# A two-layer attention kernel on one core: transposes three steps behind the scores, and the tables that follow it

## Chip, core and metric

The kernel runs on one core of one Trainium2 chip. The time is that of the device in microseconds (us) for one execution, from the first to the last thing that the core does. A core has five engines with a queue of instructions each: TensorE (PE in the rows; its loads of weights stand apart as PEld), VectorE (DVE), ScalarE (ACT), GpSimd (POOL) and SyncE (SP), which here issues nearly all DMAs. Every engine works through its own queue in order, and an instruction may wait for semaphores that other engines raise. The granted clock of TensorE was 0.993 of full speed over the profiled execution.

## What is computed

The input x is (4, 16, 16, 256) in fp32. Two attention layers are added to it, each on a group-normalised input:

```
x = x + L0(gn(x))     # 8 heads over the 16 rows, 256 tokens, relative bias, softmax over 256
x = x + L1(gn(x))     # 16 heads, 4 chunks of 64 tokens, keys of the chunk and the one before it

L0: xi = w_in . x;  q, k = w_qk . xi;  sim = (q k + bias[buckets]) / 4;  out = w_out . (softmax(sim) v), v = xi
L1: q, k, v = w_qkv . x;  attn = softmax over the chunk's 128 keys of q k / 4;  out = w_out . (attn v)
gn: mean and variance over 16 x 16 positions and 8 neighbouring channels, 32 groups
```

## The kernel before

**Units, blocks and steps.** The work is cut into 8 units: units 0 to 3 are the first layer (A) for batches 0 to 3, units 4 to 7 the second layer (B) for the same batches. A unit has 8 blocks of scores of 128 x 512. All engines run the same loop `for t in range(STEPS)`, STEPS = 8 x 8 + 12, and each puts into its own queue what the tables give to step t. Nothing but these tables sets the order in which an engine meets its instructions; semaphores set when it may go on.

**A block through the engines.** In step t TensorE makes the scores of block t (`scores`, L572 in A, L584 in B; one of two banks). VectorE adds the bias and takes the maximum (A, L952), or takes the maximum and subtracts it (B, L956 and L963). In A the maximum is subtracted on GpSimd (L362, in step t - LAG + 2). TensorE transposes a block at step t + LAG (`shifted`, L594 and L603), and ScalarE takes its exponential in the same step (L1191, PT). Two steps ahead of each block ScalarE prepares the queries: QM for every block in A (L1171), QP for every second block in B (L1182).

**A unit's end.** Its numbers in FINISH are steps counted from the unit's first block: values (L663, L673; TensorE, by halves of a unit), first transposes of the unnormalised output (L689, L693), second transposes of the normalised one (L700), output product (L706, L710). Between them ScalarE copies values out (OS, L1198, in the step of the values), VectorE divides (RC and ON, L972 to L980, in the step of the first transposes), ScalarE copies the second transposes (OT, L1206, in their step), and VectorE adds the residual one step after the output product (L989, L995). A unit of A has its ends once, a unit of B twice, for two halves. The bracketed pairs in the tables are these two halves; where a unit of A does it once, the second number counts.

**A unit's beginning.** The steps in TIMES_A, counted from the unit's first block and so negative, are those of the projection to heads XR, of Q, of K and of V (which in A is a transposition of XF). VectorE scales XR (XF, L855) in XR's step, ScalarE rounds it (XRh, L1108) in the same step, VectorE makes its low part (XRl, L866) one step later. The low parts of queries and keys (Qst and KL, L875 and L879) come one step after Q and K, the copy of V (VA, L906) one step after V. For layer B the six numbers are the transposes of X (XT), the two matmuls over groups for mean and variance (GM, GV), and Q, K, V. ScalarE writes the normalised input as a rounded XTh and a full XT (rows show XT as Sq) at GV + 1, GpSimd its low part XTl at GV + 2 (L370). ScalarE and VectorE split Q and K into high and low parts (L1134, L1139, L885); SP writes Q's and K's parts to memory and loads them back in another layout (L290, L295, L296), Q before K: store Q, store K, load Q, load K. ScalarE copies V (VB, L1150) one step after V.

**Buffers.** The score banks and the banks of the transposes are two each and alternate. F and G are one bank each: XR, K and XT use F; Q, V, GM and GV use G, in A as in B. The banks O, one for each half, hold values, both transposes and output product in turn. The subtracted blocks (SB) lie in a ring of six, the queries QM in one of four, PT holds the eight blocks of a unit.

**On ScalarE the order inside a step is:** squares and weights (first ten steps only), exponential, QM or QP, XRh, XTh and XT, high parts, VB, then OT, then OS. The two loops that give it, exponential and queries left out:

```
for step, when in enumerate((GV_B + 1, Q_B, K_B)):
    for i in due(t, when, IN_B):
        projected(i, step)
...
for i in due(t, t2[1], units_a(units)):
    normalised(i, 0)
```

## Time and profile before

| | |
|---|---|
| median of 3 runs | 175.76 us (175.17 to 175.86) |
| profiled execution | 175.02 us, span 173.1 us |
| busy | PE 150.5 (87%), DVE 110.8 (64%), ACT 108.4 (63%), POOL 53.0 (31%) |
| PE busy from 60 to 157 us | 88.7 of 97.0 us |
| PE busy from 157 us on | 10.9 of 16.1 us |
| chain that ended last | PE 59%, DVE 15%, ACT 11%, issue 7%, POOL 3%, DMA 3% |

A busy share tells how full an engine is, not whether it is waited for. For that the timeline has, ahead of an instruction, the time that its engine sat idle and who released it. The 16 us at the end are the drain: no scores are left to make, and the last unit goes through its ends one after the other. The first 60 us hold the start, in which statistics, weights and the first units share the engines.

### The profile page before, as it was taken

The numbers are of one execution on the slowest core, as the hardware profiler recorded it, in microseconds if no ns is written. First come the engines' busy times: TensorE is split into PE (matmuls) and PEld (weight loads), VectorE is DVE, ScalarE is ACT, GpSimd is POOL, SyncE is SP. The second block draws the span as 40 slices with busy tenths as digits, with TensorE's granted clock in tenths as the row PEclk, the third lists the DMA queues.
The fourth block names the chain that finished last, engine by engine and source line by source line (L and its number), as shares of the span: only waits on it lengthen the run. The fifth ranks groups of instructions, "written<-read, shape, count | busy, mean of one in ns | idle before, by whom it ended". The sixth has DMA issues, their size and how long they took to land.

```text
span 173.1 us, 4283 instructions
## 1 busy us (share of the span) xinstructions
PE 150.5 (87%) x1582; PEld 129.6 (75%) x1582; DVE 110.8 (64%) x326; ACT 108.4 (63%) x218; POOL 53.0 (31%) x106
## 2 busy tenths in 40 slices
PE   7989889769979799899989798998999898979872
PEld 7568769648868579887888677987899787868651
DVE  1645477955483776348646886799667779678220
ACT  1428417955856378737893769766976968775520
POOL 0302532959953245924590122003200200000000
PEclk9999999999999999999999999999999999999997
DMA  5409900000000000079505890369307980010101
GB/s 176 146 6 296 304 4 6 0 0 4 2 2 0 0 4 2 13 174 239 184 4 130 220 256 4 83 167 242 125 0 189 239 239 29 8 34 0 64 26 40
DMA packets 8564, 15.84 MB, mean 92 GB/s; under 512 B 1208, under 2 KB 5688, under 8 KB 7776
## 3 DMA queue, kind: packets, MB, share of 16 engines
q1 hardware_dynamic: 7984, 15.22, 32.1%
q10 hardware_dynamic: 560, 0.35, 0.7%
q8 instruction: 13, 0.21, 0.5%
q14 instruction: 7, 0.06, 0.1%
HBM read 10.31 MB, written 5.26 MB: 90 GB/s over the span
## 4 chain that ended last, share of the span: by engine, by line
PE 59%; DVE 15%; ACT 11%; issue 7%; POOL 3%; DMA 3%; ACTq 1%; DVEq 0%
PE bank L572 6%; PE bank L584 6%; PE bank L603 5%; PE bank L552 5%; PE bank L663 5%; PE bank L673 4%; PE bank L710 4%; PE bank L594 4%; PE bank L561 3%; PE bank L479 3%; DVE NM L956 3%; POOL XTl L370 3%; DMA PT<-buckets 3%; ACT Sq L1127 2%; DVE SB L963 2%
## 5 line engine op out<-in xcount | busy, mean ns | idle before, releaser
L1191 ACT ACTIVATE PT<-bank 128x512 f32<-128x512 f32 x64 | 38.2, 598 | 23.7 <-PE bank L603 11.9
L952 DVE CUSTOM_DVE_ANT_0 SB<-bank,Tk 128x256 f32<-128x256 f32 x64 | 24.5, 420 | 20.3 <-PE bank L572 20.2
L362 POOL TENSOR_SCALAR SB<-SB,NM 128x256 f32<-128x256 f32 x64 | 29.9, 481 | 13.9 <-DVE NM L952 13.5
L956 DVE TENSOR_REDUCE NM<-bank 128x4 f32<-128x512 f32 x32 | 21.9, 685 | 13.2 <-PE bank L584 13.1
L963 DVE TENSOR_TENSOR SB<-bank,NM 128x512 f32<-128x512 f32 x32 | 22.1, 692 | 1.1
L572 PE MATMUL bank<-KH,QM 128*128 128x256 f32 x64 | 21.2, 351 | 0.7 <-ACT QM L1171 0.7
L584 PE MATMUL bank<-K,QP 96*128 96x128 f32 x128 | 20.7, 284 | 0.7 <-ACT QP L1182 0.7
L1182 ACT ACTIVATE QP<-Q,con 96x512 fp32r<-96x512 f32 x32 | 21.2, 713 | 0.0
L603 PE MATMUL bank<-con,SB 128*128 128x128 f32 x128 | 19.8, 278 | 0.0
L594 PE MATMUL bank<-con,SB 128*128 128x128 f32 x128 | 19.3, 273 | 0.0
L584 PEld LDWEIGHTS bank<-K,QP 96*128 96x128 f32 x128 | 17.0, 191 | 2.4 <-ACT QP L1182 0.9
L572 PE MATMUL bank<-KL,QM 128*128 128x256 f32 x64 | 17.8, 297 | 0.0
L1171 ACT ACTIVATE QM<-Qst,con 128x256 fp32r<-128x256 f32 x32 | 16.0, 506 | 0.5 <-DVE Qst L875 0.5
L572 PEld LDWEIGHTS bank<-KH,QM 128*128 128x128 f32 x64 | 13.2, 206 | 3.7 <-issue 3.4
L594 PEld LDWEIGHTS bank<-con,SB 128*128 128x128 f32 x128 | 14.6, 140 | 0.0
L603 PEld LDWEIGHTS bank<-con,SB 128*128 128x128 f32 x128 | 13.6, 141 | 0.1
L1198 ACT ACTIVATE OS<-bank 128x256 f32<-128x256 f32 (+1 forms) x16 | 7.8, 490 | 9.1 <-PE bank L663 5.7
L572 PEld LDWEIGHTS bank<-KL,QM 128*128 128x128 f32 x64 | 13.3, 208 | 0.2
L385 POOL COPY VB<-VB 64x256 f32<-64x256 f32 x4 | 1.6, 390 | 31.5 <-ACT VB L1150 31.5
L700 PE MATMUL bank<-con,ON 128*128 128x128 f32 x24 | 5.1, 296 | 5.1 <-DVE ON L980 4.6
L663 PE MATMUL bank<-PT,VA 128*32 128x256 f32 x128 | 8.6, 385 | 0.9 <-ACT WoT L1097 0.9
L673 PEld LDWEIGHTS bank<-PT,VB 128*32 128x32 f32 x512 | 7.5, 110 | 1.8 <-ACT PT L1191 1.2
(142 smaller groups left out, 274.3 us busy)
## 6 DMA issues: line engine op xcount, KB each, us to landing
q_terms<-WQK SPq DMA_DIRECT2D x16, 128.0 KB, 2.2
k_terms<-KHL SPq DMA_DIRECT2D x16, 128.0 KB
Q<-q_terms SPq DMA_DIRECT2D x4, 512.0 KB, 5.4
K<-k_terms SPq DMA_DIRECT2D x4, 512.0 KB, 5.6
Tk<-bias_rows SPq DMA_DIRECT2D x4, 384.0 KB, 4.7
X<-x SPq DMA_DIRECT2D x4, 256.0 KB, 4.5
Q<-q_terms SPq DMA_DIRECT2D x4, 256.0 KB, 5.9
K<-k_terms SPq DMA_DIRECT2D x4, 256.0 KB, 6.1
```

Of the source, the lines that this page charges most:

```text
L362: last = nc.gpsimd.tensor_scalar(rows_of, rows_of, -1.0, NM[:, i % 2, 2 * u + nt:2 * u + nt + 1], ALU.mult, ALU.add)
L572: last = nc.tensor.matmul(s[:, nt * CH:(nt + 1) * CH], queries[:, nt * P:(nt + 1) * P], keys[:, i % 2, u // 4, :], start=(nt == 0 and keys ...
L584: last = nc.tensor.matmul(bank[S_BANK + u % 2][:, a * P:(a + 1) * P], QP[0:ROWS, c % QRING, a, g].rearrange("p v n -> p (v n)"), window, s ...
L594: last = nc.tensor.transpose(z[:, s * CH + nt * P:s * CH + (nt + 1) * P], below[:, nt * CH + s * P:nt * CH + (s + 1) * P], ident)
L603: last = nc.tensor.transpose(z[:, a * P:(a + 1) * P], below[:, a * P:(a + 1) * P], ident)
L663: last = nc.tensor.matmul(o[32 * hh:32 * hh + 32, 0:CH], VA[:, i % 3, mt, 4 * half + hh, :], PT[:, 4 * half + hh, mt * CH:(mt + 1) * CH], ...
L952: last = V.tensor_tensor_reduce(SB[:, idx % SRING, nt * CH:(nt + 1) * CH], half, Tk[:, u, nt * P:nt * P + CH], 1.0, LOWEST, ALU.add, ALU.m ...
L956: V.tensor_reduce(NM[:, i % 2, 4 * u:4 * u + 4], s[:].rearrange("p (h m) -> p h m", h=4), AX.X, ALU.max).then_inc(max_ready, 1)
L963: V.tensor_tensor(SB[:, idx % SRING, :].rearrange("p (h m) -> p h m", h=4), bank[S_BANK + u % 2][:].rearrange("p (h m) -> p h m", h=4), NM ...
L1171: A.activation(QM[:, idx % MRING, :], Qst[:, i % 2, u // 4, :].bitcast(F32), ACT.Copy, scale=con[:, C_PAIR + u % 4:C_PAIR + u % 4 + 1]).th ...
L1182: last = A.activation(QP[0:ROWS, c % QRING, :, :, v, :].rearrange("p a g n -> p (a g) n"), Q3[0:ROWS, b % 2, :, :, c * CHUNK:(c + 1) * CHU ...
L1191: A.activation(PT[:, u, :], bank[Z_BANK + u % 2][:], ACT.Exp, scale=-SCALE if is_a(i) else SCALE).then_inc(p_ready, 1)
```

## The change

LAG goes from 4 to 3: the transposes and the exponential of a block come three steps after its scores. STEPS stays. The steps of the units' beginnings and ends change with it. For unit 0 its first and second transposes and output product stand at 13, 15, 16; for units 1 to 3 values and first transposes come one step sooner, the second transposes keep their step 14, and the output product comes one step sooner, at 15. For layer B values, first transposes and output products come one step sooner, the second transposes keep their steps (the last unit's second half comes one sooner). For unit 1, K and V come ahead of Q in the queue, in units 2 and 3 too. In layer B the group matmuls, Q and V come one step later, K stays, so that Q and K share a step. The waits follow the new order in the banks: Q waits for the copy of V, V for XF and the former unit's queries, XRh and XRl for the former unit's Q in place of its K.

```diff
@@ -239,16 +239,17 @@
 
 
 
-        LAG = 4
+        LAG = 3
         STEPS = UNITS * BLK + 12
         IN_A, IN_B = range(BATCH), range(BATCH, UNITS)
-        TIMES_A = [(range(1, 2), (-6, -4, -3, -2)), (range(2, 3), (-5, -3, -3, -2)), (range(3, BATCH), (-9, -8, -8, -7))]
-        XT_B, GM_B, GV_B, Q_B, K_B, V_B = -14, -13, -12, -9, -8, -7
-
-
-        FINISH = [(IN_A, (9, 12), (13, 13), (14, 14), (16, 16)),
-                  (range(BATCH, UNITS - 1), (10, 13), (12, 15), (13, 16), (15, 18)),
-                  (range(UNITS - 1, UNITS), (10, 13), (12, 15), (13, 16), (14, 17))]
+        TIMES_A = [(range(1, 2), (-6, -4, -5, -5)), (range(2, 3), (-5, -3, -4, -4)), (range(3, BATCH), (-9, -7, -8, -8))]
+        XT_B, GM_B, GV_B, Q_B, K_B, V_B = -14, -12, -11, -8, -8, -6
+
+
+        FINISH = [(range(1), (9, 12), (13, 13), (15, 15), (16, 16)),
+                  (range(1, BATCH), (8, 11), (12, 12), (14, 14), (15, 15)),
+                  (range(BATCH, UNITS - 1), (9, 12), (11, 14), (13, 16), (14, 17)),
+                  (range(UNITS - 1, UNITS), (9, 12), (11, 14), (13, 15), (14, 16))]
 
         def units_a(units):
             return [i for i in units if i in IN_A]
@@ -479,23 +480,24 @@
                         last = nc.tensor.matmul(f[:, 0:CH], WinK[:, t, :], Xc[:, i, t, :], start=(t == 0), stop=(t == TT - 1))
                     last.then_inc(xr_done, 1)
                 if step == 1:
-                    pe.wait_ge(v_ready, v_total(i - 1))
-                    pe.wait_ge(xr_ready, i + 1)
+                    pe.wait_ge(v_ready, v_total(i))
                     for n, (w, v) in enumerate(((WQh, XRh), (WQl, XRh), (WQh, XRl))):
-                        if v is XRl:
-                            pe.wait_ge(xrl_ready, i + 1)
                         for t in range(2):
                             last = nc.tensor.matmul(f[:, t * CH:(t + 1) * CH], w[:, t, :], v[:, ::-1],
                                                     start=(n + t == 0), stop=(n == 2), skip_group_check=True)
                     last.then_inc(q_done, 1)
                 if step == 2:
+                    pe.wait_ge(xr_ready, i + 1)
                     for n, (w, v) in enumerate(((WKh, XRh), (WKl, XRh), (WKh, XRl))):
+                        if v is XRl:
+                            pe.wait_ge(xrl_ready, i + 1)
                         for t in range(2):
                             last = nc.tensor.matmul(f[:, t * CH:(t + 1) * CH], w[:, t, :], v[:],
                                                     start=(n + t == 0), stop=(n == 2), skip_group_check=True)
                     last.then_inc(k_done, 1)
                 if step == 3:
-                    pe.wait_ge(q_ready, i + 1)
+                    pe.wait_ge(q_ready, max(i, 1))
+                    pe.wait_ge(xs_ready, i + 1)
                     for m in range(2):
                         last = nc.tensor.transpose(f[:, m * P:(m + 1) * P], XF[:, m * P:(m + 1) * P], ident)
                     last.then_inc(v_done, 1)
@@ -530,7 +532,10 @@
                     last.then_inc(xt_done, 1)
                 if step == 1:
                     pe.wait_ge(agg_ready, b + 1)
-                    pe.wait_ge(v_ready, v_total(i - 1))
+                    if b == 0:
+                        pe.wait_ge(q_ready, i)
+                    else:
+                        pe.wait_ge(v_ready, v_total(i - 1))
                     nc.tensor.matmul(m[:, 0:CT], con[:, C_GRP:C_GRP + P], agg[:, :, 0], start=True, stop=True).then_inc(gm_done, 1)
                 if step == 2:
                     pe.wait_ge(mom_ready, b + 1)
@@ -862,7 +867,7 @@
                 if i == 1:
                     dve.wait_ge(part_k, 2)
                 if i >= 2:
-                    dve.wait_ge(k_done, i - 1)
+                    dve.wait_ge(q_done, i - 1)
                 V.tensor_tensor(XRl[:], XF[:], XRh[:].bitcast(F32), op=ALU.subtract).then_inc(xrl_ready, 1)
 
             def queries_keys(i, which):
@@ -1104,7 +1109,7 @@
                         if i == 1:
                             act.wait_ge(part_k, 2)
                         if i >= 2:
-                            act.wait_ge(k_done, i - 1)
+                            act.wait_ge(q_done, i - 1)
                         A.activation(XRh[:], XF[:], ACT.Copy).then_inc(xr_ready, 1)
                     if which == 1:
                         act.wait_ge(q_done, i)
```

**ScalarE, steps 29 to 31 (before).** PT is the exponential, QM and QP are queries, XTh and Sq the normalised input of unit 5, OT the copy of unit 2's second transposes.

```order
L1191 ACTIVATE PT<-bank 128x512
L1171 ACTIVATE QM<-Qst,con 128x256
L1127 ACTIVATE XTh<-bank,gnb,grs 128x256 x2
L1127 ACTIVATE Sq<-bank,gnb,grs 128x256 x2
L1191 ACTIVATE PT<-bank 128x512
L1182 ACTIVATE QP<-Q,con 96x8x64 x2
L1206 ACTIVATE OT<-bank 128x256
L1191 ACTIVATE PT<-bank 128x512
L1134 ACTIVATE WQK<-bank 128x512
```

**The same place after the change:**

```order
L1176 ACTIVATE QM<-Qst,con 128x256
L1196 ACTIVATE PT<-bank 128x512
L1187 ACTIVATE QP<-Q,con 96x8x64 x2
L1132 ACTIVATE XTh<-bank,gnb,grs 128x256 x2
L1132 ACTIVATE Sq<-bank,gnb,grs 128x256 x2
L1211 ACTIVATE OT<-bank 128x256
L1196 ACTIVATE PT<-bank 128x512 x2
L1187 ACTIVATE QP<-Q,con 96x8x64 x2
L1139 ACTIVATE WQK<-bank 128x512
```

OT of unit 2 stood a step after XTh and XT (Sq); now it stands right behind them, with the step's queries QP in front of them.

**TensorE, steps 38 to 40 (before).** K,QP are scores, con,SB a block's transposes, con,ON the second transposes of unit 3, OT,WoutK its output product, XTh and WTh the Q and then the K of unit 6.

```order
L584 MATMUL bank<-K,QP 128x128 x4
L603 MATMUL bank<-con,SB 128x128 x4
L700 MATMUL bank<-con,ON 128x128 x2
L584 MATMUL bank<-K,QP 128x128 x4
L603 MATMUL bank<-con,SB 128x128 x4
L552 MATMUL bank<-XTh,WTh 128x256 x4
L552 MATMUL bank<-XTh,WTl 128x256 x4
L552 MATMUL bank<-XTl,WTh 128x256 x4
L584 MATMUL bank<-K,QP 128x128 x4
L603 MATMUL bank<-con,SB 128x128 x4
L552 MATMUL bank<-XTh,WTh 128x256 x4
L552 MATMUL bank<-XTh,WTl 128x256 x4
```

**After, steps 37 to 39 and the start of 40:**

```order
L589 MATMUL bank<-K,QP 128x128 x4
L608 MATMUL bank<-con,SB 128x128 x4
L542 MATMUL bank<-mom,con 128x2
L589 MATMUL bank<-K,QP 128x128 x4
L608 MATMUL bank<-con,SB 128x128 x4
L705 MATMUL bank<-con,ON 128x128 x2
L589 MATMUL bank<-K,QP 128x128 x4
L608 MATMUL bank<-con,SB 128x128 x4
L711 MATMUL bank<-OT,WoutK 128x256 x2
L589 MATMUL bank<-K,QP 128x128 x4
L608 MATMUL bank<-con,SB 128x128 x4
L557 MATMUL bank<-XTh,WTh 128x256 x4
```

The output product stood behind both Q and K, two steps after the second transposes; now it stands one step after them, and Q and K follow it together.

**TensorE, steps 3 to 5 at the start (before).** KH,QM and KL,QM are scores, con,VB a transposition of layer B's weights, Part,avg means for the group norm of units 2 and 3, XRh and XRl with WQK the projections of unit 1.

```order
L572 MATMUL bank<-KH,QM 128x256
L572 MATMUL bank<-KL,QM 128x256
L572 MATMUL bank<-KH,QM 128x256
L572 MATMUL bank<-KL,QM 128x256
L594 MATMUL bank<-con,SB 128x128 x4
L450 MATMUL bank<-Part,avg 128x64
L727 MATMUL bank<-con,VB 128x128 x4
L488 MATMUL bank<-XRh,WQK 128x256 x4
L488 MATMUL bank<-XRl,WQK 128x256 x2
L572 MATMUL bank<-KH,QM 128x256
L572 MATMUL bank<-KL,QM 128x256
L572 MATMUL bank<-KH,QM 128x256
```

**After, from step 3's transposes on:**

```order
L599 MATMUL bank<-con,SB 128x128 x4
L495 MATMUL bank<-XRh,WQK 128x256 x4
L495 MATMUL bank<-XRl,WQK 128x256 x2
L502 MATMUL bank<-con,XF 128x128 x2
L577 MATMUL bank<-KH,QM 128x256
L577 MATMUL bank<-KL,QM 128x256
L577 MATMUL bank<-KH,QM 128x256
L577 MATMUL bank<-KL,QM 128x256
L599 MATMUL bank<-con,SB 128x128 x4
L451 MATMUL bank<-Part,avg 128x64
L732 MATMUL bank<-con,VB 128x128 x4
L486 MATMUL bank<-XRh,WQK 128x256 x4
```

K and V (con,XF) of unit 1 and one more block's transposes now stand ahead of the means and of the weights' transposition.

## Rows read from the trace of the kernel before

**Rows 1.** TensorE's timeline, first score matmuls: start us, us, engine, line, operation, tiles

```profile
59.12 0.39 PE L572 MATMUL bank<-KH,QM 128*128 128x256 f32 x1
...
73.51 0.47 PE L572 MATMUL bank<-KH,QM 128*128 128x256 f32 x1
...
91.43 0.75 PE L584 MATMUL bank<-K,QP 96*128 96x128 f32 x4
...
110.51 0.75 PE L584 MATMUL bank<-K,QP 96*128 96x128 f32 x4
...
129.23 0.64 PE L584 MATMUL bank<-K,QP 96*128 96x128 f32 x4
...
156.06 0.64 PE L584 MATMUL bank<-K,QP 96*128 96x128 f32 x4
```

**Rows 2.** timeline of VectorE at the end

```profile
170.55 0.43 DVE L995 TENSOR_TENSOR Y<-bank,X 128x256 f32<-128x256 f32 x1 [2.14 <-PE bank L710]
```

**Rows 3.** chain that ended last: start us, us, engine and line

```profile
20.56 1.15 PE bank L572 x4
...
71.56 1.44 PE bank L552 x12
72.99 0.87 PE bank L706 x4
73.86 0.48 PE bank L572 x4
...
76.21 1.00 PE bank L663 x16
...
129.48 0.40 PE bank L584 x4
129.88 0.46 PE bank L603 x4
```

**Rows 4.** timeline, steps 3 to 9; in brackets idle before and its releaser

```profile
26.19 0.41 DVE L866 TENSOR_TENSOR XRl<-XF,XRh 128x256 fp32r<-128x256 f32 x1
...
26.33 0.43 PE L450 MATMUL bank<-Part,avg 128*128 128x64 f32 x2 [1.15 <-DVE Part L791]
...
38.11 1.07 PE L663 MATMUL bank<-PT,VA 128*32 128x256 f32 x16 [0.88 <-ACT WoT L1097]
```

**Rows 5.** timeline of TensorE and ScalarE, steps 29 and 30

```profile
82.45 0.39 PE L572 MATMUL bank<-KH,QM 128*128 128x256 f32 x1
...
83.66 0.60 ACT L1191 ACTIVATE PT<-bank 128x512 f32<-128x512 f32 x1 [0.69 <-PE bank L594]
...
84.55 1.02 ACT L1127 ACTIVATE XTh<-bank,gnb,grs 128x256 fp32r<-128x256 f32 x2
...
86.35 0.62 ACT L1191 ACTIVATE PT<-bank 128x512 f32<-128x512 f32 x1
...
86.83 1.34 ACT L1182 ACTIVATE QP<-Q,con 96x512 fp32r<-96x512 f32 x2
...
88.05 0.38 ACT L1206 ACTIVATE OT<-bank 128x256 f32<-128x256 f32 x1
```

**Rows 6.** timeline of GpSimd at step 30

```profile
86.56 1.27 POOL L370 TENSOR_TENSOR XTl<-Sq,XTh 128x512 fp32r<-128x512 f32 x1 [1.77 <-ACT Sq L1127]
```

**Rows 7.** timeline of SP's queue for unit 4

```profile
75.78 1.74 SPq L290 DMA_DIRECT2D k_terms<-KHL  x4
...
78.14 0.58 SPq L296 DMA_DIRECT2D Q<-q_terms  x1
79.70 0.53 SPq L295 DMA_DIRECT2D K<-k_terms  x1
```

**Rows 8.** DMA issues: KB each, median us from issue to landing

```profile
Q<-q_terms SPq DMA_DIRECT2D x4, 512.0 KB, 5.4
K<-k_terms SPq DMA_DIRECT2D x4, 512.0 KB, 5.6
```

**Rows 9.** TensorE at a second transposes of unit 6

```profile
153.78 0.44 PE L700 MATMUL bank<-con,ON 128*128 128x128 f32 x2 [1.15 <-DVE ON L980]
```

## The prediction

> **What bounds the kernel now.** I read the stretches by engine first, then the gaps on TensorE with what ended them, then the chain of waits, and ScalarE's and SP's own rows where a gap ended on them. TensorE (PE) works through nearly the whole span, so an instruction that moves counts only where PE waits for it, or where a wait goes. I measure in stretches of PE's rows, S(t) being the first score matmul of step t. S(18), S(25), S(33), S(41), S(49) and S(63) start at 59.12, 73.51, 91.43, 110.51, 129.23 and 156.06 [rows 1], and the last residual add ends at 170.98 [rows 2]. Between them PE does pieces of known length: scores 0.48 in layer A and 0.40 in B, a block's transposes 0.46, each of Q, K and V of layer B 1.44, a value product 1.00, an output product 0.87 [rows 3]. For the four transposes of X or of the unnormalised output I take 0.4, for the two of the normalised one 0.2, both by rule of three from the 0.46. PE's waits are what is left in a stretch, 1 to 3 us of each.
>
> **What costs nothing by itself.** No instruction is added or taken away. PE's work is constant, and the sum is one of waits. The transposes of a block now stand two whole steps behind its scores, at least 1.7 us by rows 3, and VectorE and GpSimd need less than that; I take 0, with +1 as the other bound.
>
> **The first ten steps.** K and V of unit 1 now stand at step 3, ahead of S(4), and K's last third needs XRl. On VectorE XRl stands behind the reductions of units 2 and 3 and ends at 26.60. Before, PE waited for the same reductions, but with only their means left to do: it goes on at 26.33 [rows 4]. Now K's rest (0.3), V (0.4), S(4) (0.5) and a block's transposes (0.45) stand after XRl and before these means and the weight transposes that ScalarE waits for: they come 1.95 us later. ScalarE then works without a gap up to step 9. It has K's copy and one exponential (0.5 each) behind it already, but meets the centring on GpSimd, which now stands behind a later block. Followed to step 9, the value product that starts at 38.11 [rows 4] comes 2.9 later. Bounds: 0 (the two early pieces pay for all) and +3.5; I take +2.9. From S(10) to S(18) I take 0: V no longer waits for Qst (about 1.2, twice), but Q waits for V's copy, which VectorE makes only after that step's maxima (0.9, twice), and K for XRl (0.3, twice).
>
> **The output product behind ScalarE's normalisation: the main term.** For units 1 to 3 the output product stands one step behind the second transposes in place of two, and it needs OT. ScalarE issues in that step the exponential, QM or QP, XTh and XT, and only then OT; before, XTh and XT stood one step earlier. The exponential starts 1.2 after its step's scores (82.45 to 83.66), it and QM hold 0.9, XTh with XT 1.8 (84.55 to 86.35), the exponential alone 0.5, QP 1.22 (86.83 to 88.05), OT 0.38 [rows 5]. So OT is there 1.2 + 0.9 + 1.8 + 0.4 = 4.3 after S(22), and with QP in place of QM 5.1 after S(30) and S(38). PE wants it after one step, the two small transposes and another step: 2.15 (1.97 in layer B). The waits are 2.2, 2.95 and 3.1. What goes in return is Q's wait for XTl, which ends at 87.83 [rows 6] and kept PE 0.7 to 1.1 each time; the output product now covers it.
>
> **Q and K by way of memory.** Q and K of layer B now stand in one step, so VectorE makes both low halves in the next one, Q's first. SP stores Q, then K, then loads Q. K's stores begin at 75.78, 2.27 after S(25), and take 1.74; Q's second load is issued at 78.14, K's first at 79.70, and such loads land 5.4 and 5.6 after issue [rows 7, 8]. Q's low half now ends where K's did (2.2), its stores take 1.75, and so K's begin at 3.95 and Q has landed at 11.65. ScalarE wants it at S(30) + 1.7 = 11.0: 0.65 late. Counted from S(33) it is 12.05 against 11.1: 0.95 late. Both stand in front of OT, whose waits become 3.65 and 4.1. K lands 14.3 after S(41) and S(49), where S(48) and S(56) want it at 12.7 and 12.55. XT at steps 26, 34 and 42 needs K's low half, at 2.8, 3.15 and 3.0 of its stretch, and is due at 2.0, 1.9 and 2.85: +0.8, +1.25, +0.15.
>
> **What goes.** The layer's group means now stand where ScalarE has no QP ahead of V's copy, and a piece of PE work covers their statistics: PE's waits of 0.5 to 1.4 there, 3 us in all, go. The second transposes of layer B stand two steps behind the first, so the wait for ON, 1.15 at 153.78 [rows 9] and the same one unit earlier, goes. After S(63) there is one step less to drain: walked with rows 3 and 5 the end comes 12.3 after S(63) starts, in place of 14.9.
>
> **Sum, now minus before.** To S(10) +2.9. S(18) to S(25), 14.4 before: work 13.1 (one value product more), wait 2.2, joints 0.8, 16.1: +1.7. S(25) to S(33), 17.9: S(30) at 9.3, output product 15.1 to 16.0, a step with Q, K and a value product 4.8, 20.8: +2.9. S(33) to S(41), 19.1: S(38) at 9.45, output product 15.5 to 16.4, a step with Q and K 3.8, 20.2 (one value product less): +1.1. S(41) to S(49), 18.7: S(48) at 14.3, XTl at 16.3, the rest of Q, K and two transposes 2.15, 18.4: -0.3. S(49) to S(63), 26.8: S(56) at 14.3 and seven steps of 12.2, 26.5: -0.3. Drain -2.6. Together +5.4. The profiled execution took 175.02 us, 1.9 more than its span, so 180.4; the three runs shown have their median 0.74 above it, which gives 181.2. I say 181.0.
>
> **A rule on the loads.** The 512 KB loads took 5.4 us to land [rows 8]. The Trainium skill (DMA: Bandwidth & Descriptors, Anatomy of one DMA) puts a transfer at about 2.0 us plus its bytes at 436 GB/s; for both loads of a pair, 768 KB, that estimate is 3.8 us, and by it Q and K would be in time everywhere and the sum some 3.6 smaller. The row decides for me.
>
> **Rivals.**
> *The loads are in time.* The 0.65 and 0.95 in front of OT go, and so do the 1.6 and 1.75 before S(48) and S(56), of which XTl takes 1.3 back: -3.6, 177.4. For it: the 5.4 was seen with other traffic around. Against it: the stores move by more than the margin that the loads had. Chance 0.17, with the cases in which only the start loses less.
> *The other side: OT is not waited for.* If PE comes to the output products of steps 23, 31 and 39 no earlier than ScalarE has OT, 9.95 us go and +5.4 becomes -4.5: 170.5, and 171.2 against the median. It turns faster by over 0.5% once these three waits total under 3.6 us. For it: the gains at the second transposes and in the drain are sure. Against it: ScalarE keeps its order, and XTl, which ends later still, would take 4.4 back, which ends at 175.7, no change. Chance 0.12 for faster, 0.08 for no change.
> *PE's clock falls.* The four scores of a step took 1.15 at 20.56 and take 0.48 at 73.86 [rows 3]: at the start, between gaps, PE runs at the lower of its levels (1.2 GHz), after steady work at the higher (2.4), while the granted clock reads full in both. Waits of 3.65 and 4.1 don't occur in the loop before. If they drop it, the 3.8 us of scores, Q and K behind each take up to twice as long: up to +7.6, and 184.8 at half of that. The Trainium skill (TensorE: Matmul & The Clock Gate, Part 1: The HAM clock gate) says that an idle array goes back to half its clock. Chance 0.13.
>
> **Numbers.** Forecast 0.50, with its own range 178.6 to 183.0; the rivals as above. 176.5 to 184.5 leaves out the other side and the worst of the clock. About 0.5% (0.9 us) is what a measurement tells from no change: faster 0.12, same 0.08, slower 0.80.
>
> **What would show it.** In the profile after: three output products of layer A (bank from OT and WoutK) with PE idle 2 to 4 us before them, released by OT, and XTh and XT right in front of OT on ScalarE; S(48) or S(56) released by K's load; no wait over 0.3 at the second transposes of the last two units; the last residual add ending 12 to 12.6 after S(63) starts; the first value product starting near 41. The forecast is wrong if the waits at the three output products total under 6 us, if the first value product starts before 39.5, or if K's load never releases the scores.

## The result, and the profile after

The changed kernel takes 196.32 us (median of 4 runs, 194.83 to 197.06) against 175.46 us before (4 runs, 175.13 to 175.86): a ratio of 1.118, 95% interval 1.110 to 1.125. Slower was right; 181.0 was 15 us too low, and 196.32 lies far outside the range. The profiled execution took 195.98 us, 20.96 more than that of before, with a span of 194.0.

The page after, engines' busy time and, in 40 slices of the span, the granted clock of TensorE in tenths:

```profile
PE 159.4 (82%) x1582; PEld 137.3 (71%) x1582; DVE 111.4 (57%) x326; ACT 109.4 (56%) x218; POOL 53.3 (27%) x106
...
PEclk9958699999999978999799996999859997599999
```

The clock row of the kernel before:

```profile
PEclk9999999999999999999999999999999999999997
```

PE makes the same 1582 instructions as before and is busy 159.4 us instead of 150.5. So about 8.9 us of the 20.9 in the span are not waits at all: the same matmuls took longer. The other 12.0 are idle time of PE. The clock row shows where the matmuls were slow: behind the start it dips five times. The low digits of the start itself are no loss against the kernel before, whose pieces there are as slow under a row that reads full (last section).

Stretches of the kernel after, from S(10) to S(18), S(25), S(33), S(41), S(49), S(56) and S(63); columns are length, busy PE, PEld, DVE, ACT and POOL with counts, granted clock, DMA share, GB/s:

```profile
39.82:59.96 20.14, 18.47 (x148) 14.94 (x145) 11.33 (x46) 11.78 (x25) 12.36 (x25) 1.00 0.01 2
59.96:77.81 17.85, 15.85 (x133) 13.77 (x131) 9.10 (x43) 11.20 (x23) 8.50 (x16) 0.90 0.01 1
77.81:100.75 22.94, 18.36 (x154) 16.32 (x150) 10.77 (x45) 13.59 (x28) 9.64 (x19) 0.93 0.44 115
100.75:123.16 22.41, 17.49 (x138) 15.63 (x135) 14.57 (x31) 13.42 (x26) 3.14 (x5) 0.92 0.46 118
123.16:146.31 23.15, 19.80 (x255) 18.63 (x253) 14.94 (x33) 14.56 (x27) 3.14 (x5) 0.85 0.44 115
146.31:162.90 16.59, 13.35 (x218) 11.88 (x216) 12.20 (x21) 10.49 (x20) 1.18 (x3) 0.99 0.68 176
162.90:178.88 15.98, 15.25 (x204) 13.06 (x205) 10.74 (x18) 9.18 (x17) 0.00 (x0) 0.79 0.05 18
```

By [rows 1] the stretches S(18) to S(25), S(33), S(41) and S(49) took 14.39, 17.92, 19.08 and 18.72 before, S(49) to S(63) 26.83. They are now 3.5, 5.0, 3.3, 4.4 and 5.7 longer. The first ten steps cost 0.7 more (S(10) now starts at 39.82, before at 39.11), S(10) to S(18) 0.1, and the end after S(63) gives 1.9 back. That is the whole of it.

What PE waited for, after (us in total, times, the longest):

```profile
PE bank L711 <- ACT OT L1211: 9.0, 3, 3.8
PE bank L589 <- DMA K<-k_terms: 6.3, 2, 3.2
PE bank L530 <- DVE KHL L890: 2.5, 3, 1.5
```

The first row is the forecast's main term, three output products of layer A behind OT. Here is one of them on ScalarE and on PE; it answers to [rows 5]:

```profile
67.68 0.50 ACT L1176 ACTIVATE QM<-Qst,con 128x256 fp32r<-128x256 f32 x1
68.08 1.01 ACT L1132 ACTIVATE XTh<-bank,gnb,grs 128x256 fp32r<-128x256 f32 x2
68.98 1.02 ACT L1132 ACTIVATE Sq<-bank,gnb,grs 128x256 f32<-128x256 f32 x2
69.88 0.40 ACT L1211 ACTIVATE OT<-bank 128x256 f32<-128x256 f32 x1
...
70.33 1.96 PE L711 MATMUL bank<-OT,WoutK 128*128 128x256 f32 x4 [2.00 <-ACT OT L1211]
...
72.94 1.05 PE L599 MATMUL bank<-con,SB 128*128 128x128 f32 x4
...
78.38 0.60 PE L599 MATMUL bank<-con,SB 128*128 128x128 f32 x4
```

XTh and XT (Sq) stand right ahead of OT, as the order said they would. But read the durations on PE too: the output product's group shows 1.96, where such a group shows 1.03 to 1.13 at the full clock, and the block's transposes 1.05, where the same four take 0.60 at 78.38. The second row of the waits, at the first scores of unit 6 with the Q product behind them, shows the same:

```profile
139.68 1.12 PE L589 MATMUL bank<-K,QP 96*128 96x128 f32 x4 [3.07 <-DMA K<-k_terms]
140.60 1.07 PE L608 MATMUL bank<-con,SB 128*128 128x128 f32 x4
141.33 1.20 PE L557 MATMUL bank<-XTh,WTh 128*128 128x256 f32 x4
```

The granted clock behind each of the five long waits (length, busy PE with count, granted clock, DMA share, GB/s):

```profile
70.33:74.32 3.99, 3.99 (x16) 0.57 0.00 0
93.41:98.00 4.59, 4.59 (x23) 0.63 0.02 4
116.94:121.70 4.76, 4.76 (x24) 0.64 0.01 3
139.68:145.68 6.00, 6.00 (x29) 0.51 0.00 0
162.90:170.26 7.36, 7.23 (x86) 0.55 0.05 18
```

PE has no gap of note in these stretches and works for most of them at half of its clock, the level of 1.2 GHz. The clock does not always fall at once: behind the second and the third wait the output product still took 1.17 and 1.13, which is full pace, and only what followed it was slow. Length times missing clock (3.99 x 0.43 and so on) adds up to 1.7 + 1.7 + 1.7 + 2.9 + 3.3 = 11.3 us.

### The profile page after: what moved, and what is told of

It is laid out like the page before. It is cut to its first block, busy times and chain, and to the rows that moved or that the text cites. A ratio compares the mean times of both kernels' runs of the same rounds, so it can differ in the third digit from the quotient of the medians.

```text
span 194.0 us, 4284 instructions
## 1 busy us (share of the span) xinstructions
PE 159.4 (82%) x1582; PEld 137.3 (71%) x1582; DVE 111.4 (57%) x326; ACT 109.4 (56%) x218; POOL 53.3 (27%) x106
## 4 chain that ended last, share of the span: by engine, by line
PE 51%; DMA 19%; ACT 9%; DVE 7%; issue 5%; SPq 4%; POOL 2%; ACTq 1%; DVEq 0%
PE bank L557 8%; DMA K<-k_terms 7%; DMA Q<-q_terms 6%; PE bank L577 5%; PE bank L589 5%; PE bank L608 4%; PE bank L715 4%; PE bank L599 4%; PE bank L678 3%; SPq L291 3%; PE bank L668 3%; PE bank L480 3%; PE bank L711 3%; DMA q_terms<-WQK 3%; DMA PT<-buckets 2%
## 5 line engine op out<-in xcount | busy, mean ns | idle before, releaser
L589 PE MATMUL bank<-K,QP 96*128 96x128 f32 x128 | 22.5, 302 | 7.1 <-DMA K<-k_terms 6.3
L589 PEld LDWEIGHTS bank<-K,QP 96*128 96x128 f32 x128 | 18.6, 207 | 9.7 <-DMA K<-k_terms 6.8
L577 PE MATMUL bank<-KH,QM 128*128 128x256 f32 x64 | 20.9, 346 | 2.1 <-ACT QM L1176 2.1
L608 PE MATMUL bank<-con,SB 128*128 128x128 f32 x128 | 21.6, 297 | 0.1
L599 PE MATMUL bank<-con,SB 128*128 128x128 f32 x128 | 20.3, 283 | 0.0
L599 PEld LDWEIGHTS bank<-con,SB 128*128 128x128 f32 x128 | 15.4, 146 | 0.0
L608 PEld LDWEIGHTS bank<-con,SB 128*128 128x128 f32 x128 | 14.7, 150 | 0.4 <-issue 0.3
L1203 ACT ACTIVATE OS<-bank 128x256 f32<-128x256 f32 (+1 forms) x16 | 7.8, 488 | 11.3 <-PE bank L678 7.7
L711 PE MATMUL bank<-OT,WoutK 128*128 128x256 f32 x16 | 5.3, 461 | 9.0 <-ACT OT L1211 9.0
L715 PE MATMUL bank<-WoT,OT 128*128 128x256 f32 x32 | 9.9, 435 | 1.3 <-ACT OT L1211 1.1
L711 PEld LDWEIGHTS bank<-OT,WoutK 128*128 128x128 f32 x16 | 3.1, 213 | 10.0 <-ACT OT L1211 9.7
```

What stands on the lines that cost most here:

```text
L577: last = nc.tensor.matmul(s[:, nt * CH:(nt + 1) * CH], queries[:, nt * P:(nt + 1) * P], keys[:, i % 2, u // 4, :], start=(nt == 0 and keys ...
L589: last = nc.tensor.matmul(bank[S_BANK + u % 2][:, a * P:(a + 1) * P], QP[0:ROWS, c % QRING, a, g].rearrange("p v n -> p (v n)"), window, s ...
L599: last = nc.tensor.transpose(z[:, s * CH + nt * P:s * CH + (nt + 1) * P], below[:, nt * CH + s * P:nt * CH + (s + 1) * P], ident)
L608: last = nc.tensor.transpose(z[:, a * P:(a + 1) * P], below[:, a * P:(a + 1) * P], ident)
L715: last = nc.tensor.matmul(o[:, 0:CH], OT[:, half, g, :], WoT[:, g, :], start=(g == 0), stop=(g == 1))
```

## The experiments

All ratios are to the kernel before, run on the same chip beside them. Differences in us are between medians. Two kernels that ran on different occasions are better compared by their ratios, and where this gives another number it stands beside the first.

### Which part of the change makes the waits

**Output product one step later.**

```diff
-                  (range(1, BATCH), (8, 11), (12, 12), (14, 14), (15, 15)),
+                  (range(1, BATCH), (8, 11), (12, 12), (14, 14), (16, 16)),
```

> The changed kernel with the output product of units 1 to 3 one step later (at 16 in place of 15), all else as changed. Theory 1 (each long wait of TensorE costs its own length and then a stretch at a lower granted clock): the three waits for OT (9.0 us together) go, and with them the slow pieces behind them, some 1.5 us each; 196.3 - 9.0 - 4.5 = about 183. Rival (only the waits count, the clock falls for another reason): 187. Rival (the time is lost by the lag of three itself, and the wait comes back elsewhere): over 190.

Measured: 190.69, ratio 1.095 (1.089 to 1.101). The waits for OT in layer A are gone, and only 5.6 us came back (4.0 by the ratios) where 9.0 and more were expected. PE's waits there:

```profile
PE bank L589 <- DMA K<-k_terms: 9.4, 4, 4.6
PE bank L530 <- DVE X L994: 4.1, 3, 2.0
```

PE now stood before loads that keep a distance of their own: from S(49) to the release of S(56) by K's load it took 18.0 us, 16.6 in the changed kernel. And XT now waited for the residual, which had moved with the output product. The clock still fell, mean 0.904: other waits of about 2 us and over (2.23, 1.98, 2.08 and 4.61) had taken the place of those removed, with a low clock behind three of the four. The first two of my numbers, 183 and 187, failed in the same way, by taking a wait out of a sum without asking what is late next. The third, over 190, was right in its number and in that the wait comes back elsewhere; that the lag costs time by itself is ruled out below.

**Queries one step ahead of keys.** `Q_B` from -8 to -9 in the changed kernel.

> The changed kernel with layer B's queries projected one step sooner (Q_B at -9 in place of -8), all else as changed. Theory 1: the query terms are put and loaded before the keys' and K lands some 2.5 us sooner, so that the two waits for K (3.1 and 3.2 us) shrink to under 1 us and TensorE keeps its clock behind them; the query product now waits for XTl, about 1 us in each of four units. 196.3 - 5 - 4 + 3 = about 190. Rival (the shared step of Q and K does not matter, K is late by its own put): K's waits stay over 2.5 us and the time over 196.

Measured: 187.08, ratio 1.065 (1.054 to 1.076), 9.2 us less than the change. The four executions lie far apart, from 184.39 to 190.61, and the traced one is the fastest. PE's waits:

```profile
PE bank L557 <- issue: 4.7, 4, 1.7
PE bank L557 <- POOL XTl L371: 3.4, 4, 1.0
...
PE bank L589 <- DMA K<-k_terms: 1.2, 1, 1.2
```

K is late once, by 1.2, so the shared step was what made the load late. In its place the query product waits for XTl (3.4) and, ahead of that, for something that the view calls issue (4.7); it is most likely XTh, since in the longest case PE goes on at 90.56 and XTh ends on ScalarE at 90.46. Together this is more than the 1 us for each unit that I gave. It stands ahead of the output products and so covers those for OT. None of these waits reaches 2 us, and yet the clock fell behind two of the four places: behind 1.68 and 1.02 shortly after it (0.51 from 94.00 to 96.23), and behind 1.43 (0.57 from 113.03 to 117.00).

**Layer B's projections as before.**

```diff
-        XT_B, GM_B, GV_B, Q_B, K_B, V_B = -14, -12, -11, -8, -8, -6
+        XT_B, GM_B, GV_B, Q_B, K_B, V_B = -14, -13, -12, -9, -8, -7
```

> The changed kernel with the layer-B projections back in their steps of before (-14, -13, -12, -9, -8, -7), lag, layer-A projections and finishes as changed. XTh then stands a step ahead of OT on ScalarE, and Q a step ahead of K. Theory 1: all five waits of 2 us and over go, and the low clock with them: 174 to 178. Rival (the lag, the layer-A projections or the finishes cost time by themselves): over 180.

Measured: 181.44, ratio 1.041 (1.033 to 1.050). This one line of the change is worth 14.9 of the 21 us (13.4 by the ratios); it holds both the collision of XTh with OT and that of Q with K. The rest, 6.7 us, is in what stayed, so the rival was right and Theory 1's 174 to 178 was not: one long wait for OT is left, 2.28 at the output product of unit 4's first half, with a granted clock of 0.65 in the 4.9 us behind it.

**The same step for Q and K, in the kernel before.** `Q_B` from -9 to -8, nothing else.

> The kernel before with layer B's queries projected in the keys' step (Q_B at -8 in place of -9), all else as before. Theory 1 (Q and K in one step send the put and load of both late, K lands behind the first scores of a unit, and each such wait lowers the clock): waits for K of 2 to 3 us at the first scores of two or more units, a mean granted clock under 0.97, and 181 to 187. Rival (K's load is on time while the rest of the kernel keeps its pace): 174 to 176, since the queries no longer wait for XTl (0.73, 0.58 and 0.44 us before).

Measured: 186.19, ratio 1.068 (1.061 to 1.074): 11.3 us for one instruction group moved by one step. The time came as Theory 1 had it, the reason only in part. PE's waits:

```profile
PE bank L561 <- DVE WQK L885: 6.0, 4, 1.6
...
PE bank L584 <- issue: 2.6, 2, 1.9
PE bank L584 <- ACT QP L1182: 2.4, 2, 1.7
```

Of the 5.0 us at the scores, 1.92 and 1.69 stand at the first scores of units 4 and 5, late queries or keys; the waits of 2 to 3 us for K's load that the theory named did not come. The clock fell behind the 1.92 (0.54 in the 3.8 us from 88.25 on) and not behind the 1.69. The other 6.0 is V, which shares a bank with Q and stands one step behind it here, waiting for Q's low half; the changed kernel has V at -6 and is spared that. I had not seen this wait.

**The lag alone.** `LAG` from 4 to 3 in the kernel before.

> The kernel before with the lag of the score transposes at three in place of four, every table as before. The changed kernel with layer B's projections back still took 181.4, 6.7 us more than before. Theory 1 (the 6.7 us come from the finishes one step sooner, whose output products wait for OT, and from the layer-A projections; the lag by itself is harmless, since the scores' maximum and its subtraction are done within two steps): 174 to 176.5. Rival (a probability that comes a step sooner pushes ScalarE's other work and TensorE waits): 179 or more.

Measured: 174.77 against 174.93, ratio 0.999 (0.995 to 1.004). The lag that gives the change its name does nothing, as the prediction's 0 for it said. The loss comes with the tables.

**The lag and the finishes, without the projections.**

```diff
-        LAG = 4
+        LAG = 3
...
-        FINISH = [(IN_A, (9, 12), (13, 13), (14, 14), (16, 16)),
-                  (range(BATCH, UNITS - 1), (10, 13), (12, 15), (13, 16), (15, 18)),
-                  (range(UNITS - 1, UNITS), (10, 13), (12, 15), (13, 16), (14, 17))]
+        FINISH = [(range(1), (9, 12), (13, 13), (15, 15), (16, 16)),
+                  (range(1, BATCH), (8, 11), (12, 12), (14, 14), (15, 15)),
+                  (range(BATCH, UNITS - 1), (9, 12), (11, 14), (13, 16), (14, 17)),
+                  (range(UNITS - 1, UNITS), (9, 12), (11, 14), (13, 15), (14, 16))]
```

> The kernel before with the lag of three (which by itself changed nothing: 174.8 against 174.9) and the finishes of the changed kernel, projections of both layers as before. It parts the 6.7 us that the changed kernel lost even with its layer-B projections put back: Theory 1 (they come from the finishes: OT of unit 4's first half behind XTh on ScalarE, 2.3 us of wait and a low clock behind it, and 1.1 us more of OT in unit 6): 178 to 181. Rival (they come from layer A's order of keys and values ahead of queries): 173 to 175, since the waits for ON are gone.

Measured: 179.44 against 174.25, ratio 1.034 (1.028 to 1.040), so 5.2 us are the finishes. The wait named is there, with slow groups behind it (the output product's group shows 2.08):

```profile
124.42 2.08 PE L711 MATMUL bank<-WoT,OT 128*128 128x256 f32 x4 [2.28 <-ACT OT L1207]
```

The other 1.5 of the 6.7 would be layer A's order of K and V ahead of Q, but the intervals of the two kernels (1.033 to 1.050, 1.028 to 1.040) overlap, so the size of this part is not settled. The two traces place it at the start: from S(0) to S(10) the kernel with this order took 25.50 us and the one without it 22.47; from S(10) on they differ by 0.6.

### What the clock costs

**The five waits filled.** Ahead of each long wait PE gets matmuls that compute nothing, into the bank that it is about to overwrite.

```diff
+            def keep_going(where, count):
+                for n in range(count):
+                    nc.tensor.matmul(where[:, 0:P], avg[:], avg[:], start=True, stop=True)
...
                 if step == 2:
+                    if is_a(i) and i:
+                        keep_going(bank[O_BANK + 1], (0, 8, 15, 12)[i])
                     pe.wait_ge(ot_ready, n + 1)
...
                 elif u == 0:
+                    if i > BATCH + 1:
+                        pe.wait_ge(subb_ready, idx - BATCH * BLK - 1)
+                        keep_going(bank[S_BANK], 13)
                     pe.wait_ge(k_loaded, 32 * (i - BATCH + 1))
```

> The changed kernel with matmuls that compute nothing (avg by avg, 128 x 128) put ahead of TensorE's waits for OT at the output products of units 1, 2 and 3 (8, 15 and 12 of them) and ahead of its wait for K's load at the first scores of units 6 and 7 (13 each), each group a little shorter than the wait was. The work waited for comes no sooner. Theory 1 (the clock falls because TensorE stands still, and this is some 8 us of the loss): the granted clock stays near its level of before (mean 0.97 or more against 0.91) and the time is 186 to 189. Rival (the clock fell for another reason, power or the order of the work): the mean clock stays under 0.93 and the time 195 or more.

Measured: 187.80, ratio 1.075 (1.067 to 1.084). The four executions took 186.62, 186.81, 188.79 and 376.86 us; the median counts them all and the ratio only the first three. So the gain over the changed kernel is about 8 us: 8.5 by this median, 9.5 by that of the three, 7.4 by the ratios, with more work on PE and nothing done sooner by it. The mean clock was 0.957, 0.958 and 0.991 in the three, above the rival's 0.93, though two of them are below the 0.97 that I had asked for. The kernel before itself had 0.941 to 0.993 beside them: the mean also holds the start (last section), so it is a poor measure, and the clock behind each wait a better one.

The execution of 376.86 stays unexplained. Its trace shows PE busy for 98% of the span, at less than even the lower pace (the transposes of a block take 1.40, where 0.60 is full pace and 1.07 that of the lower level), under a granted clock that reads 1.00. A profile of the filled kernel at its usual speed was therefore taken with a single execution:

> One look at the changed kernel with TensorE's five long waits filled by matmuls that compute nothing, for a profile of it at its usual speed (186.6 to 188.8 us). Theory 1: the granted clock holds through all five places and the pieces behind them last as long as before (0.48 and 0.98 us rather than 0.78 and 1.9). Rival: the pieces behind the filled waits are as slow as in the changed kernel, and the 8 us came from something else.

Measured: 192.23, not the 186.6 to 188.8 that was wanted. It stood at 42.05 at S(10), 2.2 behind the changed kernel, and its clock was at half from 40 to 45 us (0.50), ahead of all the filled places. From S(10) to the end of the span it took 148.3 us, the changed kernel 154.2 and the kernel before 134.0; from 45 us on its mean clock is 0.99, where the changed kernel has 0.92, and it did not fall at any of the five filled places. The place of the wait for K:

```profile
136.80 2.73 PE L689 MATMUL bank<-avg 128*128 128x128 f32 x23
140.09 0.67 PE L589 MATMUL bank<-K,QP 96*128 96x128 f32 x4 [0.56 <-DMA K<-k_terms]
140.59 0.62 PE L608 MATMUL bank<-con,SB 128*128 128x128 f32 x4
140.97 0.72 PE L557 MATMUL bank<-XTh,WTh 128*128 128x256 f32 x4
```

PE stands at the same point for 3.3 us (136.80 to 140.09; 3.07 in the changed kernel), and behind it the three groups take 0.67, 0.62 and 0.72 in place of 1.12, 1.07 and 1.20.

**Pauses in the kernel before.** At steps 44 and 52 GpSimd, which has little to do there, works on a buffer of its own, and PE waits for it ahead of the next step's scores.

```diff
+        PAUSES, LONG = (44, 52), 11
...
+            def pause(t):
+                k = PAUSES.index(t)
+                pool.wait_ge(s_done, t)
+                for n in range(LONG):
+                    pool.wait_ge(paused, k * LONG + n + 1)
+                    nc.gpsimd.tensor_scalar(scratch[:], scratch[:], -1.0, mhalf[:, 0:1], ALU.mult, ALU.add).then_inc(paused, 1)
...
+                if idx - 1 in PAUSES:
+                    pe.wait_ge(paused, LONG * (PAUSES.index(idx - 1) + 1) + 1)
```

> The kernel before, in which TensorE waits at two places, ahead of the scores of steps 45 and 53, for eleven operations of GpSimd on a buffer of their own (0.48 us each for 128 x 256, 5.3 us together, begun at the start of the step before, which takes 2.5 to 3 us): two waits of some 2.5 us, all else as before. Theory 1 (a wait costs its length and then a stretch at a lower granted clock): the pieces behind each wait last about 1.7 times as long for 4 to 6 us, and the kernel takes 5 + 3 = 8 us more, 182 to 184. Rival (a wait costs its own length at most, and later waits for ON and QP shrink by it): 178 to 180 with the clock as before.

Measured: 191.17, ratio 1.102 (1.095 to 1.109). The pauses were longer than meant, 7.60 and 5.91: the eleven operations took 6.2 and began late. So the expected time doesn't hold. What it shows: 16.9 us lost where the waits are 13.5, and half the clock behind both of them, 0.51 in the 4.2 us behind the second. Behind the first (length, busy PE, granted clock, DMA share, GB/s):

```profile
125.32:131.00 5.68, 5.68 (x83) 0.52 0.01 3
```

**The same pauses with PE kept at work** (30 and 23 matmuls of avg by avg ahead of the two waits).

> The kernel before with the same two pauses of 7.6 and 5.9 us (eleven operations), of which TensorE spends all but the end on matmuls that compute nothing (30 and 23 of 128 x 128, 0.24 us each). All that waits for TensorE comes as late as with the empty pauses; only TensorE doesn't stand still. Theory 1 (it is the standing still that lowers the clock, and the low clock that costs what the kernel with empty pauses, 191.2, lost beyond the 13.5 us of wait): 187 to 188.5, clock as before. Rival (the rest is lost to work that comes late behind the pauses, not to the clock): 190 or more.

Measured: 187.01 (186.86 to 187.13), ratio 1.070 (1.063 to 1.077), 4.2 us less than with empty pauses (5.5 by the ratios), as Theory 1 had it. Everything waited as long; only PE did not stand still. The traces put the gain where the theory has it: from S(45) to S(53) it took 25.31 us with empty pauses and 23.43 with filled ones, and from S(53) to the end of the span 36.97 and 35.12. So the low clock cost 1.9 us for each wait, some quarter of what these pauses cost. The clock did not stay up everywhere, though: it fell once ahead of both pauses, at a place that the edit doesn't touch, which is shown below.

**Short pauses** (three operations in place of eleven).

> The kernel before with the two pauses at steps 45 and 53, made of three operations of GpSimd in place of eleven (the eleven took 6.2 us and gave waits of 7.6 and 5.9 us), so waits of some 3.1 and 1.4 us. Theory 1 (a wait costs its length and a stretch at the low clock): the first lowers the clock for some 5 us, the second perhaps not; 4.5 + 2.6 = 7 more at most, less what later waits give back: 179 to 182. Rival (what follows a wait is slow only after the long ones): 178 and the clock as before.

Measured: 179.31, ratio 1.026 (1.019 to 1.033). The heads of the two places here, and of the first place filled (the first row is its filler):

```profile
121.69 1.12 PE L597 MATMUL bank<-K,QP 96*128 96x128 f32 x4 [3.01 <-POOL scratch L387]
...
141.47 0.66 PE L597 MATMUL bank<-K,QP 96*128 96x128 f32 x4 [1.32 <-POOL scratch L387]
```

```profile
118.89 6.86 PE L635 MATMUL bank<-avg 128*128 128x128 f32 x60
126.65 0.66 PE L597 MATMUL bank<-K,QP 96*128 96x128 f32 x4 [0.90 <-POOL scratch L387]
```

The same four score matmuls are slow behind 3.01 us of idle time, and at full pace behind 1.32, or behind 0.90 with PE at work before it. 4.9 us were lost for 4.3 of wait. Theory 1's 179 to 182 holds; the time alone would not tell it from the rival's 178, the clock behind the first wait does (0.56 in 3.8 us).

**How long must a wait be?** No single length parts the cases. In the traces, past the first 40 us, PE has 15 waits of 1.9 us and over that are not filled (seven kernels, one execution of each). Behind 14 of them the granted clock was 0.51 to 0.72 in the 3.6 to 7.4 us that followed. Behind the other one, in the kernel with the output product one step later, it stayed at 1.00:

```profile
92.25 0.66 PE L589 MATMUL bank<-K,QP 96*128 96x128 f32 x4 [2.23 <-DMA K<-k_terms]
```

Behind shorter waits it fell too, but not each time. In eleven of the kernels the matmuls of the group means wait 1.24 us for V's copy. Here they are in the kernel before and in the one with filled pauses, ahead of the first pause, with the value product that follows:

```profile
98.66 0.35 PE L534 MATMUL bank<-agg,con 128*128 128x2 f32 x2 [1.23 <-ACT VB L1150]
...
100.39 1.07 PE L663 MATMUL bank<-PT,VA 128*32 128x256 f32 x16
```

```profile
96.91 0.35 PE L547 MATMUL bank<-agg,con 128*128 128x2 f32 x2 [1.24 <-ACT VB L1168]
...
98.85 1.93 PE L681 MATMUL bank<-PT,VA 128*32 128x256 f32 x16
```

The instructions are the same and the waits alike, yet the clock held in the first execution and was at 0.50 for 3 us and more in the second. It fell at such a place in five of the eleven traces. What else decides it, no run here shows.

### Can the kernel before be bettered

Three versions try what was sound in the change, the gap of two steps between layer B's first and second transposes, so that ON is ready.

> The kernel before with layer B's second transposes of the second half, its output products and those of the last unit's second half one step later ((14, 17) and (16, 19); last unit (14, 17) and (15, 18)), so that ON is ready when the second transposes come, as in the changed kernel. Theory 1: the waits for ON before the last two units' second transposes (1.15 us each) go and nothing comes in their place: 173.5 to 174.5 against 174.8. Rival (the output product or the next unit's value product waits in its turn, and the last unit ends a step later): 175 to 177.

Edit: units 4 to 6 `(10, 13), (12, 15), (14, 17), (16, 19)`, last unit `(10, 13), (12, 15), (14, 17), (15, 18)`. Measured over 12 runs: 173.92 against 174.93, ratio 0.996 (0.992 to 0.9995). The waits for ON there are gone, but two others came, so each side of the expectation was right in part:

```profile
PE bank L673 <- DVE Y L995: 1.9, 4, 0.8
...
PE bank L584 <- DMA K<-k_terms: 1.4, 1, 1.4
```

> The kernel before with layer B's second transposes one step later, as in the version that ran at 0.996 of it, but units 4 to 6's output products left in their steps (15, 18), so that the next unit's value product does not wait for Y (0.80 us in two units there). Theory 1: the waits for ON are gone and no wait for Y comes: 172.8 to 174 against 174.5. Rival (the output product, now one step behind the second transposes, waits for OT instead, or the time given back is taken by K's load): 174.5 or more.

Edit: as above with units 4 to 6's output products left at `(15, 18)`. Measured: 174.27 against 174.43, ratio 1.000 (0.996 to 1.004): the wait for Y went, and the output products waited for OT instead (2.5 us in four places). That is the rival's wait, at a time 0.2 under its 174.5; Theory 1's 172.8 to 174 was missed.

> Lag of three, projections of both layers and layer A's finishes as before; layer B's finishes as in the changed kernel but with the first half's output product one step later (units 4 to 6: (9, 12), (11, 14), (13, 16), (15, 17); last unit (9, 12), (11, 14), (13, 15), (14, 16)), so that it does not wait for OT behind XTh. Theory 1: the waits for ON go (2.3 us and more), no new wait of over 1 us comes, and the drain is 1 to 2 us shorter: 171.5 to 173.5. Rival (K's load, the residual or the next value product waits in turn): 174.5 to 176.

Edit: lag 3, layer A's finishes and all projections as before, layer B's as the expectation has them. Measured: 176.05 against 174.25, ratio 1.010 (1.004 to 1.016): slower by 1%, where Theory 1 had a gain. The waits for ON gave way to waits for VB (2.8, of which 1.6 stood before), OT (2.5) and QP (1.2, of which 0.7 stood before). Only the first of the three beats both kernels, and by so little (its interval ends at 0.9995) that it is hardly told from none.

## Why the prediction was wrong, and where it was right

**The step that failed: no term for the clock in the sum.** "PE's work is constant, and the sum is one of waits" was the premise, and it did not hold: PE was busy 8.9 us longer with the same instructions. The prediction saw the mechanism ("If they drop it, the 3.8 us of scores, Q and K behind each take up to twice as long: up to +7.6"), but made it a rival with a chance of 0.13, for waits of 3.65 and 4.1 alone, and left it out of the +5.4. The trace shows it behind all five waits of 2 us and over, also behind the 2.00 at 70.33, and for 4.0 to 7.4 us of work each, 11.3 us in all. Of the 15.5 us by which the sum was short (+5.4 against +20.9) this is the greater part. Removed by itself the low clock is worth about 8 us in the changed kernel and about 4 in the kernel with two pauses. The first is less than the 11.3 of the windows; most likely part of what a faster PE gains is waited away again. The Trainium skill (TensorE: Matmul & The Clock Gate, Part 1: The HAM clock gate), cited there for an idle array's half clock, has the trace on its side (0.51 to 0.64 behind the five waits): by that rule the sum should have held a price for each long wait.

**Also too low: K's load.** I had K landed 14.3 after S(41) and S(49), waits of 1.6 and 1.75; it was there after 16.5 and 16.6, and the waits were 3.07 and 3.24. SP's rows for unit 6, with S(41) at 123.16:

```profile
125.80 1.74 SPq L291 DMA_DIRECT2D q_terms<-WQK  x4
127.58 2.68 SPq L291 DMA_DIRECT2D k_terms<-KHL  x4
...
132.72 0.58 SPq L297 DMA_DIRECT2D K<-k_terms  x1
```

K's stores begin 4.4 after S(41), where I had 3.95, and take 2.68, where I took about 1.75 from [rows 7]. The last load is issued at 132.72, 9.6 after S(41), and the scores are released at 139.68, 7.0 later, where I added the 5.6 of [rows 8]. For unit 7 the stores begin 5.2 after S(49) and take 1.84, and the scores are released 6.9 after the last load's issue. So the 5.6, a median over four units, was too low both times, and the 1.75 is the row of one unit. The prediction's other figure, the estimate of 3.8 us from the Trainium skill (DMA: Bandwidth & Descriptors, Anatomy of one DMA), is by that section one for transfers issued from GpSimd; these were issued from SyncE, and 7.0 and 6.9 are far from it. The clock behind these two waits (2.9 + 3.3) and the later load (1.5 + 1.5) together are 9.2 of the 10.8 by which S(41) to S(63) missed its -0.6 (it was +10.2).

**The waits for OT: right.** Forecast 2.2, 3.65 and 4.1, together 9.95; measured 2.00, 3.77 and 3.19, together 8.96. The waits of XT for K's low half, forecast as 0.8, 1.25 and 0.15, were 0.81, 1.47 and 0.25. S(18) to S(41) was still forecast 6.1 too short (+5.7, measured +11.8), 5.1 of which is the low clock behind these three waits.

**The start: the sign failed, the size may hold.** The first value product started at 38.82, not near 41, so the forecast's own sign ("before 39.5") spoke against it. But this execution reached S(0) 0.74 us sooner than before (15.14 against 15.88). From S(0) to S(10), the changed kernel and the four others with its order in layer A took 24.7 to 26.7, ten with the order of before 22.5 to 23.3. One execution of each was too few to read this term of +2.9 off the changed kernel alone.

**The second transposes and the drain: right in direction.** PE's waits for V's copy at the group means, 1.6 us in two places before, no longer appear. No wait of over 0.3 stood at the last two units' second transposes, save the last one of all. The last residual add ended at 191.87, 13.0 after S(63), where 12.3 was forecast and 14.9 was before.

**The rivals.** "The loads are in time" was wrong: they were later still. The other side needed OT not to be waited for, and it was. Of my three conditions for being wrong one was met, the start.

## What to carry to other kernels

Price a new wait on TensorE at its length plus what follows it: behind 14 of 15 waits of 1.9 us and over the clock fell to half for most of the next 4 to 7 us of work, 1.5 to 3.3 us of missing clock each; filling the waits gave back some 1.9 us for each in one kernel and about 8 us for five in the other. Shorter waits are not safe either: behind 1.2 to 1.7 us it fell in some executions and held in others. A step moved onto the step of another producer costs twice: in a queue that works in order, the new neighbour comes first (XTh ahead of OT), and what the two share (a bank, a DMA queue) makes the second late. And a wait taken out of a sum gives back less than its length if a load with its own pace stands next.

## What the runs showed of the hardware

- Idle time and clock: behind 1.32 us of idle time the scores' group took 0.66, behind 3.01 us 1.12, and the group of the output product behind 2.00 us 1.96. But it took 0.66 behind 2.23 us too, and behind 1.24 us the clock fell to 0.50 in some executions. Matmuls that compute nothing in the same gap keep the pace; they gave back about 8 us of 196.3.
- The granted clock can read full where TensorE is slow. Near the start the same score matmuls took 0.41 us each in the kernel before, where the clock reads 1.00 (15.88 to 24.00), and in the kernel with filled pauses, where it reads 0.50 (14.10 to 22.00); behind the start they take 0.28. From S(0) to S(10) these two took 23.23 and 23.26 us. In the execution of 376.86 us it reads 1.00 throughout. So compare durations, and not the mean clock of an execution alone.
- Behind longer waits the low clock lasted longer in the changed kernel (7.36 us behind 3.24), but not in step with them: 5.7 us behind 7.60.
- The four stores of a unit's K took 1.84 to 1.87 us in three units of the changed kernel and 2.68 in unit 6, 1.72 to 1.82 before; and K was there 7.0 and 6.9 us after its last load was issued (units 6 and 7), not 5.6 [rows 8].
